# Taylor-attention row sums of four pairs in one bank with one reciprocal chain, and one loop order for each engine

## The reference, cut to what matters

```python
x = x + 0.5 * low_rank_ffn(layernorm(x))          # half A
x = x + softmax_attention(layernorm(x))           # half A: 16 heads of 8, causal, layer norm inside
x = x + 0.5 * low_rank_ffn(layernorm(x))          # half A
x = x + 0.5 * moe(layernorm(x))                   # half B: 8 experts, top 2
x = x + taylor_attention(layernorm(x))            # half B: 16 heads, causal
x = x + 0.5 * moe(layernorm(x))                   # half B
...
def taylor_attention(h):                          # q, k: 16 features a head; v: 64
    attn = (1 + s + s * s / 2) * mask             # s = q.k / 4
    y = (attn @ v) / (attn.sum(-1) + 1e-12)
```

## Time and profile before

| | us |
|---|---|
| median of 3 runs | 1573.84 |
| lowest and highest | 1571.40, 1575.87 |
| span of the profiled execution | 1575.1 |
| prologue (A alone) | 126.5 |
| one turn of the loop (seven) | 184.3 |
| epilogue (B alone) | 158.4 |

### The profile page before, as it was taken

How to read it: one execution, slowest core, us unless ns; L and a number is a source line. 1 busy time by engine, 2 the same in 40 slices (tenths; PEclk the granted TensorE clock), 3 DMA queues, 4 the chain that set the end, 5 groups by cost and what they waited for, 6 DMA issues and landing times. The chain is left out here.

```text
span 1575.1 us, 30631 instructions
## 1 busy us (share of the span) xinstructions
PE 1282.2 (81%) x9276; PEld 748.3 (48%) x9322; DVE 1158.5 (74%) x3626; ACT 697.8 (44%) x1186; POOL 301.8 (19%) x794
## 2 busy tenths in 40 slices
PE   4677789876997879977899769978799778996687
PEld 2335445553455534654456534556346554464135
DVE  2834897769966798658977699667986589775575
ACT  4243265442743446342654426533464426642342
POOL 0020033100430014200331003310142103310130
PEclk8787999988998999989899899988999899998798
DMA  3000200002000010002000020000100010000100
GB/s 100 21 1 7 53 10 2 9 15 54 1 2 16 21 41 2 1 15 50 12 2 9 13 57 1 2 16 21 41 2 2 15 44 18 2 8 1 40 1 7
DMA packets 37085, 28.94 MB, mean 18 GB/s; under 512 B 7872, under 2 KB 36224, under 8 KB 36928
## 3 DMA queue, kind: packets, MB, share of 16 engines
q1 hardware_dynamic: 36928, 26.91, 6.7%
HBM read 5.78 MB, written 2.10 MB: 5 GB/s over the span
## 5 line engine op out<-in xcount | busy, mean ns | idle before, releaser
L627 ACT ACTIVATE wts<-bank 128x512 f32<-128x512 f32 x320 | 182.4, 602 | 109.4 <-PE bank L1091 76.0
L587 ACT ACTIVATE probs<-bank 128x512 f32<-128x512 f32 x320 | 176.0, 605 | 107.6 <-PE bank L1004 107.4
L736 DVE TENSOR_REDUCE bmax<-bank 128x4 f32<-128x512 f32 x320 | 207.4, 679 | 10.8 <-PE bank L985 10.7
L983 PE MATMUL bank<-kpad,q0a 128*128 128x384 f16 (+3 forms) x512 | 142.9, 337 | 71.7 <-DVE kpad L728 37.5
L937 PE MATMUL bank<-lnTB_hi,pairs 128*128 128x512 f16 x448 | 149.3, 418 | 24.3 <-DVE wts L835 11.4
L1114 PE MATMUL bank<-wts,v 128*64 128x512 f32 (+3 forms) x1024 | 152.1, 439 | 0.0
L825 DVE SCALAR_TENSOR_TENSOR lnB<-bank,comb,lnB 128x128 f32<-128x128 f32 x448 | 125.7, 343 | 29.1 <-PE bank L1067 25.6
L504 POOL TENSOR_TENSOR spareB<-neghalf 1x1 f32<-1x1 f32 x192 | 46.7, 243 | 503.4 <-DVE wts L855 503.4
L855 DVE TENSOR_SCALAR wts<-wts 128x1024 f32<-128x1024 f32 (+1 forms) x192 | 128.4, 686 | 19.2 <-ACT wts L627 17.4
L1067 PEld LDWEIGHTS bank<-ew,yT 128*128 128x128 f32 x1024 | 131.7, 191 | 22.0 <-issue 7.4
L1091 PE MATMUL bank<-q1a,kpad 96*128 96x512 f16 (+3 forms) x512 | 122.7, 319 | 23.8 <-ACT wts L627 22.5
(11 more groups left out here) (151 smaller groups left out, 2180.0 us busy)
## 6 DMA issues: line engine op xcount, KB each, us to landing
q1a<-wts SPq DMA_DIRECT2D x96, 64.0 KB, 2.1
yT<-wts SPq DMA_DIRECT2D x96, 64.0 KB, 2.0
q0a<-probs SPq DMA_DIRECT2D x96, 32.0 KB, 1.8
probs<-probs SPq DMA_DIRECT2D x96, 32.0 KB, 1.8
xA<-x_dram SPq DMA_DIRECT2D x8, 256.0 KB, 2.8
out_dram<-res SPq DMA_DIRECT2D x8, 256.0 KB, 2.9
wo<-wo_dram SPq DMA_DIRECT2D x1, 512.0 KB, 3.4
ew<-ew_dram SPq DMA_DIRECT2D x1, 512.0 KB, 4.3
```

Of the source, the lines that this page charges most:

```text
L587: act.activation(probs[:, g % 2, u * S:(u + 1) * S], ps[:, :], ACT.Exp).then_inc(A.act, 1)
L627: act.activation(wts[:, p % 2, u * S:(u + 1) * S], ps[:, :], ACT.Square, bias=1.0, scale=FEAT ** -0.5).then_inc(Bh.act, 1)
L736: dve.tensor_reduce(bmax[:, u * NT:(u + 1) * NT], ps[:, :].rearrange("p (b k) -> p b k", k=P), AX.X, ALU.max).then_inc(A.dve, 1)
L983: mm(ps[:, c0:c0 + n_keys], q0a[:, g, qt * P:(qt + 1) * P], kpad0[:, g * GH + j, 0:n_keys], start=True, stop=False)
```

## The change

**Row sums.** `GP = 4` pairs share one bank. The constant `ones` (32 equal columns) becomes `column[:, k, :]`: 32 columns of which only column k is 1. Pair p multiplies with `column[:, p % 4, :]` and so puts its sums in row p % 4 of each 32; the other rows get zeros added. The four pairs add up in `denB`: the first of them starts the sum, the last one stops it and signals `den_done`. The transposed bank then holds four sums side by side.

**The chain.** A new step `recip.g` runs the chain once for pairs 0 to 3 and once for pairs 4 to 7. It has the same nine operations, seven of them four times as wide (64 x 64 in place of 64 x 16). `spread` becomes four matrices, one for each pair of a group, so that `scale p` picks its rows of `rrows`.

**The steps.** `recip.0` stands after `den.3` and `recip.1` after `den.7`. `scale.0` to `scale.3` come after it between the squares of pairs 5 and 6, `scale.4-7` all behind `num.7`. `out1.0` now has pairs 0 to 3 and stands before `num.5`; `out1.1` has pairs 4 to 7.

**The orders.** `LOOP` is a string for each of PE, DVE, ACT, POOL and SP, and each engine runs its own merge of the two lists. The lists themselves are shared, so each half keeps its order everywhere.

**Set-up.** `spreadf` is cleared by DVE and filled by eight small DMAs behind the weights; DVE makes the bf16 `spread` of it in `split_weights`, where ACT made it before.

```diff
-OUT1_PAIRS = (range(NPAIR - 2), range(NPAIR - 2, NPAIR))
+OUT1_PAIRS = (range(GP), range(GP, NPAIR))
...
-    pad1.0 v1.2-3 pad1.1-3 sq.0-7 den.0 sq.8-9 num.0 sq.10-11 scale.0 den.1 sq.12-14 num.1 sq.15-17 scale.1
-    den.2 sq.18-19 num.2 sq.20-22 scale.2 den.3 sq.23-24 num.3 sq.25-27 scale.3 den.4 sq.28-29 num.4 sq.30
-    scale.4 sq.31 den.5 sq.32-34 num.5 scale.5 sq.35 den.6 sq.36-39 num.6 scale.6 den.7 num.7 scale.7
-    out1.0-1 stat.2 centre.2 split.2 router.1 gate.2-3 route.1 expert.8-15 store""")
...
+    pad1.0 v1.2-3 pad1.1-3 sq.0-7 den.0 sq.8-9 num.0 sq.10-11 den.1 sq.12-14 num.1 sq.15-17
+    den.2 sq.18-19 num.2 sq.20-22 den.3 recip.0 sq.23-24 num.3 scale.0 sq.25-27 scale.1 den.4 sq.28-29 scale.2
+    num.4 sq.30 scale.3 sq.31 den.5 sq.32-34 out1.0 num.5 sq.35 den.6 sq.36-39 num.6 den.7 recip.1 num.7 scale.4-7
+    out1.1 stat.2 centre.2 split.2 router.1 gate.2-3 route.1 expert.8-15 store""")
...
-                part({"A": i + 1, "B": i}, order_loop)
+                part({"A": i + 1, "B": i}, weave(ORDER_A, ORDER_B, name))
...
-            def den1(it, p, step):
+            def recip(it, g, step):
...
-                chB.then(dve.reciprocal(rrec[:, :], dsum[:, :]))
+                chB.then(dve.reciprocal(rrec[:, :, :], dsum[:, :, :]))
...
             def den1(it, p, step):
-                if p:
-                    pe.wait_ge(den_read, it * NPAIR + p)
+                if p == GP:
+                    pe.wait_ge(den_read, it * 2 + 1)
...
-                            last = mm(denB[row:row + 32, kt * P:S], ones[:, 0:32],
-                                      wts[:, p % 2, c0:c0 + WIDTH[kt]], start=kt < 2, stop=kt >= 2)
-                last.then_inc(den_done, 1)
+                            last = mm(denB[row:row + 32, kt * P:S], column[:, p % GP, :],
+                                      wts[:, p % 2, c0:c0 + WIDTH[kt]], start=kt < 2 and p % GP == 0,
+                                      stop=kt >= 2 and p % GP == GP - 1)
+                if p % GP == GP - 1:
+                    last.then_inc(den_done, 1)
```

126 lines of the change are left out of this document (82 added, 44 removed).

## The result

The changed kernel takes 1638.85 us (median of 4 runs, 1638.71 to 1640.12), and the kernel before takes 1574.86 us beside it. The ratio is 1.0409, with an interval of 1.0396 to 1.0423. The change costs 64 us, where the prediction had it gain 40. The profiled execution has a span of 1637.1 us.

What follows compares the result with a forecast made beforehand. PE 81% and DVE 74% busy, the bound varying by stage, mostly PE. Seven turns of -5.0 us give -35, epilogue -6, prologue +0.5: span 1534.6, median 1533 us (-2.6%); own range 1515 to 1550, widest 1496 to 1568.

Steps and rivals of the forecast that it cites:

- all up to the first square: Turn's start through row maxima: later PE start, part got back by earlier transfers; +0.5 us a turn, bounds -1 and +2.
- first pairs, pairs 2 to 7, the two chains' own waits: B's attention: -3.5 us in pairs 0 and 1, -0.8 in pairs 2 to 7, +0.3 of waits at each recip.
- second MoE stage: End of a turn: separate engine orders save 1.8 us of its 2.1 us idle time and similar waits in the loop.
- epilogue: B alone after the last turn: six chains gone, shorter mask waits; gain of 6 us, between 3.4 and 10.
- prologue: Half A alone before the loop: eight small transfers and one 512-column DVE copy add 0.5 us.
- The head: Turn's start: PE starts 1.1 us later for A's lnA, waits 0.6 for ACT's copy; +1.7 us before part is got back.
- my rival of a slower clock: First pairs of B: small PE gaps keep the clock low, +3 us a turn, 1590 us; chance 0.09.
- that risk for the loop: Attention's tail: recip.1 before scale.4 to scale.7, out1.1 with four pairs; +0.3 us a turn in PE-bound surroundings.
- I had 3.5: One widened reciprocal chain on DVE: 3.5 us instead of 2.99, bounds 3.0 and 4.8.
- I had 16.9: DVE's loss per turn: eight chains of 23.9 us become two of 7.0, so 16.9 us less, from 143.8 to 127.
- One table load less a turn: ACT's order keeps six of seven table loads, 1.28 us each; worth nothing on the path.
- the signs that I named: First square to square 14: 21 to about 15 us, clock over 0.85; PE busy per turn falls 2 to 3 us.

Runs made afterwards that it cites:

- router_first: The changed kernel with B's router.0 put back ahead of A's norm.0 on TensorE and ScalarE, gates still late: 1638.62 us, ratio 1.0412.
- gates_first: The changed kernel with B's router, gate.0, gate.1 and route.0 put back ahead of A's up0 and down0, A's norm.0 still before the router: 1620.64 us.
- tail_but_pool: The changed kernel with the whole tail order of VectorE, TensorE and ScalarE as before, only GpSimd's order left as changed: 1604.86 us, ratio 1.0194.
- pv_first: The changed kernel with A's pv0.3 put back ahead of B's split.2 on TensorE and VectorE: 1662.38 us, ratio 1.0540.

## Why the prediction was wrong

Its terms for a turn, and what each was:

| term | predicted | measured |
|---|---|---|
| all up to the first square | +0.5 | +5.7 |
| first pairs, pairs 2 to 7, the two chains' own waits | -3.5 - 0.8 + 0.3 + 0.3 = -3.7 | -2.4 |
| second MoE stage | -1.8 | +5.2 |
| a turn | -5.0 | +8.5 |
| epilogue | -6 | +3.5 |
| prologue | +0.5 | -1.2 |

**The head is the first failed step.** "So PE starts about 1.1 us later, and waits 0.6 us for ACT's copy ahead of the up-projection: +1.7 us", with a part got back, and +0.5 in all. I priced what TensorE's queue does at the moved steps, and there I was near: it starts 1.1 us later and waits 0.39. I did not price whose work the moved steps had been hiding. A's projections before the gate mean that the gates, their way over ScalarE and the routing on VectorE have nothing beside them. My text lists the two rows at 690 us and none of the routing. To put the router back alone gives nothing, as `router_first` shows. What I left out, the late gates and the routing behind them, is by itself about half of the head's loss (18.2 of 37.6 us in `gates_first`).

**The second failed step is the -1.8 for the second MoE.** "PE, DVE and ACT can pass each other where a single order held all of them" is an argument for freedom and not a row; it had no lower bound, and I wrote none. In `tail_but_pool` the old places are back and 34 us with them. The clue was in the order of VectorE: `centre.2` of B ahead of `pv0.2` of A, the copy that frees the bank for the next product.

**The middle was right in kind.** The stage of the first pairs was bound by VectorE and cost clock as well; with the chains cut, 3.3 us a turn come back, and the clock with them (0.90 and 1.00 in its windows, against 0.82). I had 4.3. The changed kernel's stage 781 to 802 is at 0.92, so my rival of a slower clock did not come here. But I took the gather as a shorter chain alone. It also moves 3.8 us of TensorE's work out of the end of the attention and leaves there a serial piece as long as before. I had that as +0.3.

**The epilogue is the third failed step.** -6 was taken between 3.4 and 10 from VectorE's freed time. With the chains cut and all else as it was, it is -1.8. The gather turns it into +3.5: one chain and four scales in a row behind the last pair, with nothing of A beside them, and a slower clock in out1.1 (0.69 granted over its 5.47 us). I named that risk for the loop ("it costs nothing or little" in surroundings bound by TensorE) and did not ask it again for the one place where these surroundings are missing.

**Sizes that held.** The second chain of the turn, as the timeline of VectorE in the changed kernel shows it:

```profile
844.50 0.72 DVE L897 STREAM_TRANSPOSE d<-bank 128x512 f32<-128x512 f32 x1 [1.81 <-PE bank L1140]
...
845.72 0.55 DVE L906 RECIPROCAL rrec<-dsum 64x64 f32<-64x64 f32 x1
...
847.41 0.71 DVE L911 STREAM_TRANSPOSE rrows<-rsplit 128x512 bf16<-128x512 bf16 x1
848.04 0.65 DVE L790 COPY oT<-bank 128x512 f32<-128x512 f32 x1
```

That is 3.54 us from the first transpose to the copy behind the chain; I had 3.5. VectorE lost 14 us a turn; I had 16.9, because I counted the chain with its gaps, which busy time leaves out (summed over the timeline, the chains take 22.8 us before and 7.2 after), and because the centring of B came back stretched (below). One table load less a turn was worth nothing, as said: `router_first` has eight loads a turn, two more than the changed kernel, and its time. Of the signs that I named, the additions from the first square to square 14 take 15.1 us in place of 18.0, the stretch from the end of the first MoE to the first square is 0.7 us longer, and TensorE waits 0.3 us for a chain at `scale.0`, all as said; but TensorE's busy time in a turn rose by 4.7 us where I had it fall by 2 to 3. My widest range ended at 1568, and the slower rival at 1590 was the wrong mechanism. All my bounds above zero came from waits of TensorE that I could see in one queue.

## What to carry to other kernels

When a change reorders queues, price each moved step twice: what it waits for in its own queue, and what chain on other engines it had been covering or had stood ahead of. A swap that looks like "one step earlier" can cost a large part of the serial chain that it uncovers. A freed engine gives back only what TensorE was waiting for (here 3.3 us a turn for 9 us of VectorE); batching a latency chain pays only if the consumers of the batch are not lined up behind it at the end, so give the turn that runs without its neighbour an order of its own. And parts of an order interlock: putting one back can cost more than leaving all (`pv_first`), so test the parts together and alone before naming one.
